# VectorE's carry moved from 11 to 7 chunks behind its one-hot, and the group addition from chunk 6 to chunk 12 of a group

## The reference, cut to what matters

```python
seg  = dst * R + edge_type                      # R = 65
sums = segment_sum(x[src], seg).reshape(N, R, F_in)
cnt  = segment_sum(ones, seg).reshape(N, R, 1)
agg  = sums / maximum(cnt, 1.0)
conv = einsum('nri,rio->no', agg, W_rel) + x @ W_root + bias
h    = conv + x @ W_res + b_res
h    = relu((h - h.mean(0)) * rsqrt(h.var(0) + EPS) * gamma + beta)
out  = layernorm(x + h)                          # over the features
```

## Time and profile before

| | us |
|---|---|
| median of 3 runs | 2467.42 (2466.01 to 2476.47) |
| the profiled execution | 2460.68 |
| its span, first to last instruction | 2459.0 |
| TensorE busy | 1856.0 (75%) |
| VectorE busy | 1649.4 (67%) |
| GpSimd busy | 1484.2 (60%) |
| ScalarE busy | 884.4 (36%) |

### The profile page before, as it was taken

The page is one execution under the profiler, slowest core; times in us unless marked ns, Lnnn a source line. Parts: engine busy times, 40 slices in busy tenths (PEclk is TensorE's granted clock), DMA queues, the critical chain, the costliest instruction groups (busy, mean ns, idle before and its releaser), DMA issues.

```text
span 2459.0 us, 36813 instructions
## 1 busy us (share of the span) xinstructions
PE 1856.0 (75%) x10368; PEld 1606.9 (65%) x10368; DVE 1649.4 (67%) x3958; ACT 884.4 (36%) x1651; POOL 1484.2 (60%) x1582
## 2 busy tenths in 40 slices
PE   5787776778688767778777778677767777877888
PEld 3566666667677666666666666666656666666677
DVE  7776675677567567668667667567656766765865
ACT  4333333333333333333333333333333333333333
POOL 6666666666666656666665666666656666666650
PEclk8898899899899889888888889889988988988899
DMA  8534433334443333443343344343333334344333
GB/s 272 155 88 91 90 88 88 90 88 90 92 90 89 88 87 87 90 96 83 89 94 84 86 91 89 84 92 86 88 84 90 88 88 90 88 89 90 86 76 106
DMA packets 244745, 233.79 MB, mean 95 GB/s; under 512 B 27097, under 2 KB 239491, under 8 KB 243907
## 3 DMA queue, kind: packets, MB, share of 16 engines
q0 software_dynamic: 223056, 203.79, 37.1%
q1 hardware_dynamic: 21491, 27.60, 3.6%
HBM read 218.48 MB, written 12.80 MB: 94 GB/s over the span
## 4 chain that ended last, share of the span: by engine, by line
PE 52%; DVE 20%; issue 14%; another core or an unknown queue 10%; ACT 2%; DVEq 2%; DMA 0%; ACTq 0%; SPq 0%; POOL 0%; POOLq 0%
PE ps L636 30%; PE tb L660 19%; DVE onehot L1011 9%; DVE agg L1026 5%; ACT agg L763 2%; PE tb L567 2%; DVEq L350 1%; DVE same L950 1%; DVE tmph L1043 1%; DVEq L1026 0%; DVE lst L1219 0%; DMA eth<-in_edge_type_dram 0%; DVE agg L1243 0%; PE tb L617 0%
## 5 line engine op out<-in xcount | busy, mean ns | idle before, releaser
L532 POOL DMA_INDIRECT xg<-xtab,srcT x1545 | 1457.6, 943 | 885.7 <-PE ps L636 478.4
L636 PE MATMUL ps<-onehot,xg 128*128 128x456 f32 x3126 | 1152.8, 465 | 569.8 <-DVE agg L1026 495.8
L1011 DVE TENSOR_SCALAR onehot<-iota,segT,vT 128x456 fp32r<-128x456 f32 x1563 | 1158.3, 744 | 493.3 <-PE ps L636 400.5
L763 ACT ACTIVATE agg<-ps 128x390 f32 (+1 forms) x1563 | 840.7, 538 | 1514.9 <-PE ps L636 1160.6
L660 PEld LDWEIGHTS tb<-agg,wsb 128*128 128x128 f32 x6370 | 1014.0, 203 | 60.5 <-issue 1.5
L636 PEld LDWEIGHTS ps<-onehot,xg 128*128 128x128 f32 x3126 | 570.2, 220 | 717.7 <-issue 695.8
L660 PE MATMUL tb<-agg,wsb 128*128 128x138 f32 x6370 | 1034.5, 294 | 1.4 <-issue 1.4
L1026 DVE SCALAR_TENSOR_TENSOR agg<-ps,agg 128x65 f32 x1514 | 395.3, 261 | 8.4 <-ACT agg L763 8.1
L1043 DVE SCALAR_TENSOR_TENSOR tmph<-iota,lastg,tb 128x138 f32<-128x138 f32 x49 | 17.6, 358 | 213.9 <-remote 147.6
L950 DVE SCALAR_TENSOR_TENSOR same<-ps,rel 128x1088 bf16<-128x1088 f32 (+3 forms) x96 | 146.0, 1521 | 17.0 <-PE tb L567 15.8
L567 PE MATMUL tb<-same,identb 128*128 128x512 bf16 x416 | 113.0, 397 | 5.2 <-DVE same L950 5.1
(11 more groups left out here) (132 smaller groups left out, 329.1 us busy)
## 6 DMA issues: line engine op xcount, KB each, us to landing
xg<-xtab,srcT POOLq DMA_INDIRECT x1545
xtab<-agg SPq DMA_DIRECT2D x4, 1536.0 KB
hinit<-H SPq DMA_DIRECT2D x1, 3125.0 KB
agg<-in_x_dram SPq DMA_DIRECT2D x4, 768.0 KB, 7.0
out_dram<-agg SPq DMA_DIRECT2D x6, 448.0 KB, 3.0
dsth<-in_dst_dram SPq DMA_DIRECT2D x23, 64.0 KB
eth<-in_edge_type_dram SPq DMA_DIRECT2D x23, 64.0 KB
srcr<-in_src_dram SPq DMA_DIRECT2D x12, 64.0 KB
```

The lines of the kernel that those rows point to most:

```text
L532: pool.indirect_dma_start(out=xg[c % RING][:], out_offset=None, in_=xtab.bitcast(F32R), in_offset=bass.IndirectOffsetOnAxis(ap=srcT[t % 2] ...
L636: ins = nc.tensor.matmul(ps[c % NRB][:, 0:OW], rows, onehot[o][:], start=(part == 0), stop=(part == 1))
L763: nc.scalar.activation(agg_group(g)[:, :, bass.ds(off, n)], ps[c % NRB][:, 0:n * R].rearrange("f (n r) -> f r n", r=R), ACT.Copy).then_inc ...
L1011: nc.vector.tensor_scalar(onehot[o][:].rearrange("p (a b) -> p a b", a=3), iota3[:, :, 0:IW], segT[t % 2][:, k:k + 1], vT[t % 2][:, k:k + ...
```

## The change

`CARRY_LAG` is the distance in chunks between the one-hot that VectorE writes and the carry that it adds right behind it. It goes from 11 to 7. `add_group(p-2)` is called behind the one-hot of chunk 12 of the group and no longer behind that of chunk 6. The places of `columns_of` and `offsets_of` in the tile move from 117 to 114 and from 126 to 122.

```diff
-CARRY_LAG = 11
+CARRY_LAG = 7
-DVE_COLS = 117
+DVE_COLS = 114
-DVE_OFFS = 126
+DVE_OFFS = 122
@@ for c in range(NCH): (VectorE's loop)
-                if p >= 2 and i == 6:
+                if p >= 2 and i == 12:
                     add_group(p - 2)
```

## The result

The changed kernel takes 2520.06 us (2517.38 to 2521.33, 4 runs) against 2469.81 us before (4 runs): ratio 1.0209, interval 1.0179 to 1.024. It is **2.1% slower**, clear of no change, though the interval doesn't settle whether it is more than 2%. 2285 us were predicted, and 2475 us was the upper end. Its profiled execution has a span of 2519.3 us, 60 us more than before.

A forecast was written before the change was run, and what follows sets the result against it. Engines waiting for each other, chiefly TensorE for VectorE's late carry, were taken as the bound. 2460.7 - 165 - 185 + 165 = 2276 us for the profiled execution, so a median of 2285 us, range 2150 to 2475.

The forecast's parts named there:

- (b): TensorE's waits for VectorE's carry outside group starts: shorter with the lag of 7, -185 us (bounds -80 to -270).
- (a): Group starts: with the group addition at chunk 12 VectorE's blocked wait goes, -165 us (bounds -120 to -214).
- (c): Compares: carry, compare, sum, aggregate and evacuation form a closed loop of 4.2 us per two chunks, +165 us (+60 to +360).
- (d): The rest (moved columns and offsets, one-hots, gathers, clock): 0; 12 x 1 us if columns and offsets aren't covered.
- The change does nothing: Late increments, not VectorE's order, set the pace; TensorE waits equally long elsewhere: 2465 us, 10% chance.
- The slower rival: Compare loop: late increments in nearly every turn make it 6.8 us, about 2540 us in all; 15% chance.

The follow-up runs named there:

- m3: Kernel before the change with every second gather left out from chunk 18 on: 1899.9 us.
- e4: Changed kernel with every second gather left out from chunk 18 on: 1813.0 us.
- e2: Kernel before with only the group addition moved from chunk 6 to chunk 12, lag still 11: 2402.39 us, ratio 0.975.
- j3: Kernel before with only the group addition moved to chunk 12, run again in a later set: 2431.56 us, ratio 0.9844.
- e3: Changed kernel with TensorE's sums of compares four chunks later: 2401.15 us, ratio 0.9742.

## Why the prediction was wrong, by its steps

**The step that failed is (b)**, with (a) behind it. It read the carry as late because of its place on VectorE, and took TensorE's increments as late by a fixed 2.6 us now and then. Moving the carry one chunk nearer to the increment would then save up to 1.1 us of each wait, -185 us in all. The place was right and the lateness was not fixed: it grew from 734 to 966 us (single cases from 2.6 to 4.9 us), and groups 1, 2 and 4 went from 48.5, 49.1, 48.1 to 46.9, 47.7, 48.6 us, where near 43 us was forecast. (a) and (b) were to save 350 us together; what the change saves outside the compare stretches is 72 us. All nine kernels that ran with late increments at the full number of gathers, with lags of 7 and 11, with 100% or 51% of the products, and with full or short rows, have these three groups between 45.9 and 49.1 us. Where the lateness is absent, terms (a) and (b) are there: 3.6 to 4.5 us per group between m3 and e4, about half of the 350 us / 48 groups = 7.3 us of the sum. That lateness takes up what the schedule gives back is read from these two comparisons. Why it grows with the change isn't known.

**(a)** was right on VectorE (213.9 to 11.9 us, below 20 as forecast) and wrong as a saving: in e2 it is worth 62 us, in j3 39 us, not 165.

**(c)** was right in mechanism and near in size. The turn is 4.1 us (4.2 forecast), TensorE's wait for line 950 112.2 us (above 100 forecast), the compare stretch 37.0 us (34 to 40), the third group 55.7 us (near 55). The stretch costs 10.5 us per tile more, 126 us over 12 tiles, against 165 in the sum, and 7.0 us per third group net; 55 us for late increments inside the ring were too much: 12 late evacuations fall there in the 12 tiles, 29 us by the count of above.

**(d)** The columns and offsets weren't tried alone. VectorE's idle time before its first reads for them (lines 977 and 995) went from 26.5 to 33.4 us and from 11.5 to 14.3 us, inside the 12 us of the term. GpSimd's bound of 1865 us was set too low, since the gap behind every gather counts: where it is the limit the loop takes 1545 x 1.245 = 1923 us.

**The rivals.** "The change does nothing" had the true reason for the missing gain, late increments that set the pace, and the sign that pointed to it, four groups of unequal work that take equal time. It was given 10%, and it was taken to exclude (c). The case that came is both together: almost no gain from (a) and (b), and the price of (c). My sum treated the terms as independent of one another, so no rival stood there. The slower rival named the wrong reason, a turn of 6.8 us.

**What stays open.** The lateness needs the gathers at their full number, and it needs a condition that changed between sets while the program did not. What this condition is, and how a gather delays the increments of another engine, no run here shows. The ring of 12 was not tried under it, nor were gathers with fewer increments of their semaphore. No version tried beats both kernels by more than e2 and e3 do (2402 and 2401 us beside 2464); without lateness the change is the fastest measured with all gathers, by 0.4%, and e2's schedule was seen there only with half of the waits or with the shorter ring (2041 and 2046 us).

## What to carry to other kernels

Groups with unequal work and equal times say that something outside the counted work sets the pace; find it before adding up savings, and give "no saving, full cost" a place among the cases. When a wait in an in-order engine is moved closer to what it waits for, look for the loop that it closes through the others, and count the loop's links: here compare, sum, aggregate, evacuation and carry gave 4.2 us on paper and 4.1 us on the chip, and four chunks of distance opened it (ratio 1.0209 to 0.9742). A lead over a producer is set by two numbers together, the place of the wait and the place of the consumer, and one is not to be changed without the other.

## What the hardware showed that was not expected

- The same program took 2452 to 2476 us in some sets of runs and 2036 to 2043 us in others, each steady to 0.7% within a set. In the slower condition TensorE's increments reached the waiting engines late in 340 to 452 of 1563 chunks; in the change the latest was 8.3 us behind the aggregate's recorded end (1990.61 to 1998.94). In the faster condition 2 to 6 chunks are late.
- The condition can be told from a trace even where nothing is late. A gather increments its semaphore 16 times, 25008 times in all. In the faster condition the change's trace records 24996 of these, in the slower one 7131. The run with memsets has 12348 of 12656 in the faster condition and 5037 in the slower one, at the same time and lateness. Whether the missing increments arrived together or only weren't recorded, the traces don't show.
- With every second gather left out, the lateness was 5 to 44 us and the time the same in both conditions (1853.51 and 1851.9 us). Rows per gather (16 or 128) and bytes per row (512 or 1024) hardly mattered (lateness 949 and 928 us, beside 966 us).
- A gather of 16 rows occupies GpSimd for 842 ns and one of 128 rows for 943 ns, so 89% of its time doesn't depend on the rows:

```profile
L532 POOL DMA_INDIRECT xg<-xtab,srcT x1545 | 1300.2, 842 | 1070.1 <-PE ps L636 509.6
```
